# Cross-attention and a 16-expert feed-forward layer on one core: fewer early weight pieces per batch, the last batch's add moved up, b2 copies written as flat runs

## The chip, the cores and the metric

One Trainium2 chip, one of its cores. The metric is the device time of one execution in microseconds, the median of several runs. A core has five engines: TensorE (PE in the profile, its weight loads PEld), VectorE (DVE), ScalarE (ACT), GpSimd (POOL) and SyncE (SP), which here only issues transfers; 16 DMA engines move the data.

## The reference

Eight batches of 100 tokens of width 512, a context of 722 rows for each batch, everything in float32:

```
x = x + attend(layernorm(x), ctx)      # attend: h = gelu(x ctx^T) * (x ctx^T), then h ctx
n = layernorm(x)
e = argmax(n @ router_w), gate = sigmoid(logit of e)          # one expert of 16 for a token
x = x + gate * (gelu(n @ w1[e] + b1[e]) @ w2[e] + b2[e])
```

w1 is 16 x 512 x 1024, w2 is 16 x 1024 x 512: 4 MB an expert, 64 MB in all.

## The kernel before

**Attention stage.** A loop over the eight batches b. Each has its context in two layouts, transposed (`ctxT_a`, `ctxT_b`) and plain (`ctx_main`, `ctx_rest`), each cut into two parts: the first 384 rows (chunks 0 to 2) and the other 338 (chunks 3 to 5). Parts are numbered n = 2b and 2b + 1 and rotate through three places for each layout in the tile `area`. TensorE runs for a batch: `hidden` (L319, six chunks), in between the transposes and logits of the batch before (L341, L347), its routing (L354, L355, L359), then `attention` (L331, three matmuls of the first part, three of the second) and, between these, the transposes of the next normalised x (L308). VectorE adds the residual (`add_x2`, L549), takes its statistics (`x2_stats`), and routes. When a batch is routed, GpSimd writes its rows to memory (`put_rows`, L813).

**Transfers.** SyncE issues nearly all of them from one queue in the order of its program; a wait on it holds back all that stands behind. In batch b it waits for the places of the two transposed parts 2b + 3 and 2b + 4 (L227), of the plain parts 2b + 3 (L234 to L236) and 2b + 4 (L231), and of x of batch b + 3 (L218). Between these it issues pieces of the weights of the first four experts, which have places of their own (`W_early`) and wait for nothing: a piece is half of w1 or of w2 of an expert, 1 MB, 8 KB in each of 128 partitions (`load_w`, L242); 16 of them make up four experts, taken in order from the iterator `early`, two in each batch. In batch 1 it also issues b1 and the four b2 copies (L276): `b2_q`, a table of 4 x 16 x 129 floats in memory, each of its four quarters read into 32 partitions of `b2s`. The fifth place for weights lies in `area` and is filled after the last context; experts 5 to 15 follow as places come free (`s_w1_used` and so on).

**Expert stage.** Work comes in units of 32 tokens of one expert. The first four units ("early", experts 0 to 3) are chosen after batch 6; their rows are gathered from memory by GpSimd (L869), signalled by `s_er[0]` to `s_er[3]`. Then each expert has one unit that always runs (`must`) and as many more as it needs (`more`, a loop over a count read at run time). For a unit VectorE normalises and transposes the rows (`fetch`, L664 to L669), TensorE runs `first_layer` (L376, 32 matmuls; L385), VectorE turns the result and adds b1 (`turn`, L692, `add_bias`, L697), ScalarE applies gelu (L495), TensorE runs `second_layer` (L398, 64 matmuls), VectorE finishes (L685) and GpSimd scatters the rows (L826). The order on VectorE around the first units is written out by hand: wait for `s_tab_e`, `s_bias` and `s_er[0]`, `fetch` of unit 0, then `add_x2` and `x2_stats` of batch 7, then `turn` of unit 0. On TensorE: `first_layer` of expert 0, the transposes and logits of batch 7, `first_layer` of expert 1, and so on.

Of the kernel before, what the change touches and what calls it, by code (L numbers as in the profile page):

```python
# [14 lines left out]
P = 128  # L15
NB, T, D, S = 8, 100, 512, 722
E, F = 16, 1024
# [8 lines left out]
U = 32  # L26
# [50 lines left out]
def build(nc, x, ctx_main, ctx_rest, ctxT_a, ctxT_b, router, w1, b1, w2, b2, consts, out):  # L77
    rows = nc.dram_tensor("rows", (TOK, Q * ROW), F32).ap()
    rows_q = rows.rearrange("n (j c) -> (n j) c", c=ROW)
    b2_q = nc.dram_tensor("b2_q", (Q, E, P + 1), F32).ap()  # L80
    out_q = out.rearrange("b t (j d) -> (b t j) d", j=Q)

    with ExitStack() as stack:
        def sb(name, shape, dt=F32):
            return stack.enter_context(nc.sbuf_tensor(name, shape, dt))
# [11 lines left out]
        b1s, b2s = sb("b1s", [P, E, KF]), sb("b2s", [P, E, P + 1])  # L97
# [38 lines left out]
        def ctxT_part(n):  # L136
            at0, w = PART * (n % 3), (SA, S - SA)[n % 2]
            return area[:, at0:at0 + KD * w].rearrange("p (k s) -> p k s", k=KD)

        def ctx_part(n):  # L140
            at0 = PART * (3 + n % 3)
            return area[:, at0:at0 + PART].rearrange("p (c d) -> p c d", c=3)
# [72 lines left out]
        @block.sync  # L215
        def _(sp):
            def load_x(b):
                sp.dma_start(xin[0:XS, b % XR, :], x[b][0:XS]).then_inc(s_x[b % XR], 16)  # L218
                if b == 0:
                    return  # L220
                load_x_rest(b)

            def load_x_rest(b):
                sp.dma_start(xin[XS:T, b % XR, :], x[b][XS:T]).then_inc(s_x[b % XR], 16)

            def load_ctxT(n):
                sp.dma_start(ctxT_part(n), (ctxT_a, ctxT_b)[n % 2][n // 2]).then_inc(s_T[n % 3], 16)  # L227

            def load_ctx(n):
                if n % 2 == 0:  # L230
                    sp.dma_start(ctx_part(n), ctx_main[n // 2][:, 0:3, :]).then_inc(s_C[n % 3], 16)  # L231
                else:
                    rest = ctx_rest[n // 2]
                    sp.dma_start(ctx_part(n)[:, 0:2, :], ctx_main[n // 2][:, 3:5, :]).then_inc(s_C[n % 3], 16)  # L234
                    sp.dma_start(ctx_part(n)[0:CS, 2, :], rest[0:CS]).then_inc(s_C[n % 3], 16)
                    sp.dma_start(ctx_part(n)[CS:CW[-1], 2, :], rest[CS:CW[-1]]).then_inc(s_C[n % 3], 16)  # L236

            def load_w(e, piece):
                w, src = (W1, w1) if piece < 2 else (W2, w2)
                n = (KD, KF)[piece // 2] // 2  # L240
                h = piece % 2
                sp.dma_start(w[e % SLOTS][:, n * h:n * h + n], src[e][:, n * h:n * h + n]  # L242
                             ).then_inc(s_w[e % SLOTS][piece], 16)

            sp.dma_start(con[:, 0:C_ONE], consts[:, 0:C_ONE]).then_inc(s_con0, 16)
            load_x(0)
            load_ctxT(0)
            sp.wait_ge(s_zero, 2)
            load_x_rest(0)
            load_ctxT(1)  # L250
            load_ctx(0)
            load_ctx(1)
            load_x(1)
            sp.dma_start(con[:, C_ONE:C_ALL], consts[:, C_ONE:C_ALL]).then_inc(s_con, 16)
            for k in range(KD):
                sp.dma_start(rw[U * k:U * k + U], router.rearrange("(g r) k e -> k r g e", g=Q)[k]).then_inc(s_con, 16)
            sp.dma_start(b2_q[:, :, 0:P], b2.rearrange("e (j d) -> j e d", j=Q)).then_inc(s_b2q, 16)
            sp.dma_start(b2_q[:, :, P:P + 1], consts[0:Q, C_ONE:C_ONE + E].unsqueeze(2),
                         allow_slow_non_contiguous=True).then_inc(s_b2q, 16)
            load_ctxT(2)  # L260
            load_ctx(2)
            load_x(2)
            early = iter([(e, piece) for e in range(SLOTS - 1) for piece in range(4)])
            for b in range(NB):
                if 2 * b + 3 < 2 * NB:
                    sp.wait_ge(s_xps[0], b + 1)
                    load_ctxT(2 * b + 3)
                load_w(*next(early))
                if 2 * b + 4 < 2 * NB:
                    sp.wait_ge(s_xps[1], b + 1)  # L270
                    load_ctxT(2 * b + 4)
                if b == 1:
                    sp.dma_start(b1s[:, :, :], b1).then_inc(s_bias, 16)
                    sp.wait_ge(s_b2q, 32)
                    for j in range(Q):
                        sp.dma_start(b2s[U * j:U * j + U], b2_q[j].unsqueeze(0).to_broadcast([U, E, P + 1])  # L276
                                     ).then_inc(s_bias, 16)
                if 2 * b + 3 < 2 * NB:
                    sp.wait_ge(s_att0, b + 1)
                    load_ctx(2 * b + 3)  # L280
                load_w(*next(early))
                if 2 * b + 4 < 2 * NB:
                    sp.wait_ge(s_att, b + 1)
                    load_ctx(2 * b + 4)
                if b + 3 < NB:
                    sp.wait_ge(s_x2, b + 1)
                    load_x(b + 3)
            sp.wait_ge(s_xps[1], NB)
            load_w(SLOTS - 1, 0)
            load_w(SLOTS - 1, 1)  # L290
            sp.wait_ge(s_att, NB)
            load_w(SLOTS - 1, 2)
            load_w(SLOTS - 1, 3)
            for e in range(SLOTS, E):
                sp.wait_ge(s_w1_used, e - SLOTS + 1)
                load_w(e, 0)
                load_w(e, 1)
                sp.wait_ge(s_w2a_used, e - SLOTS + 1)
                load_w(e, 2)
                sp.wait_ge(s_w2b_used, e - SLOTS + 1)  # L300
                load_w(e, 3)
# [226 lines left out]
        def _(dve):  # L528
# [16 lines left out]
            def add_x2(b):  # L545
                dve.wait_ge(s_att, b + 1)
                if b > 1:
                    dve.wait_ge(s_row[b % 2], 16 * (b // 2))
                nc.vector.tensor_tensor(xw[:, b % 2, :, 0:P].rearrange("p g (k r) -> p g k r", k=KD),  # L549
                                        xin[0:T, b % XR, :].rearrange("p (k g r) -> p g k r", k=KD, g=Q),  # L550
                                        p_att[0:T, :].rearrange("p (k g r) -> p g k r", k=KD, g=Q), ALU.add
                                        ).then_inc(s_x2, 1)

            def x2_stats(b):
                dve.wait_ge(s_x2, b + 1)
                nc.vector.bn_stats(bn_t[:, :], xw[:, b % 2, :, 0:P]).then_inc(s_bnt, 1)
                dve.wait_ge(s_bnt, b + 1)
                nc.vector.bn_aggr(ag_t[:, :], bn_t[:, :]).then_inc(s_agt, 1)
                dve.wait_ge(s_agt, b + 1)
                nc.vector.tensor_scalar(ve_t[:, :], ag_t[:, 1:2], EPS, None, ALU.add).then_inc(s_vet, 1)  # L560
                nc.vector.tensor_copy(xw[:, b % 2, :, P + 1:P + 2], ag_t[:, 0:1].unsqueeze(1).to_broadcast([T, Q, 1]))
# [58 lines left out]
            def early_slots():  # L620
                first = p_tab.rearrange("p (e n) -> p e n", e=E)[:, 0:EARLY, 0]
                dve.wait_ge(s_tabps, NB - 1)
                nc.vector.tensor_scalar(tab_e[:, :], first, far_col, None, ALU.add).then_inc(s_tab_e, 1)
                nc.vector.tensor_scalar(tab_before, p_tab, far_col, None, ALU.add).then_inc(s_tab0, 1)
# [37 lines left out]
            def fetch(j, v, row, index, e):  # L662

                nc.vector.tensor_scalar(tb[:, :], row[:, 0:P], row[:, P + 1:P + 2], row[:, P + 2:P + 3],  # L664
                                        ALU.subtract, ALU.mult).then_inc(s_tb, 1)
                dve.wait_ge(s_tb, v)
                nc.vector.transpose(xT[:, :], tb[:, :]).then_inc(s_xT, 1)  # L667
                nc.vector.transpose(rT[:, :], row[:, 0:P]).then_inc(s_rT, 1)
                nc.vector.tensor_copy(lin[:, bass.ds(ring(j), 1)], index)  # L669
# [19 lines left out]
            def turn(v):  # L689

                dve.wait_ge(s_h, v)
                nc.vector.transpose(hb0[:, :], p_h[:, 0:KF * U]).then_inc(s_hc, 1)  # L692
# [40 lines left out]
            fix_early()  # L733
            early_slots()

            dve.wait_ge(s_tab_e, 1)
            dve.wait_ge(s_bias, 16 + 16 * Q)
            dve.wait_ge(s_er[0], 16)
            fetch(0, 1, grow[:, 0, :], tab_e[:, 0:1], 0)
            add_x2(NB - 1)  # L740
            x2_stats(NB - 1)
            turn(1)
            residual(0, 1, grow[:, 0, :], 0)
            dve.wait_ge(s_er[1], 16)
# [213 lines left out]
```

## Time and profile before

| | |
|---|---|
| median of 3 runs | 353.48 us (353.39 to 358.01) |
| the profiled execution | 353.11 us, span 351.0 us |
| busy in the span | PE 267.0 us, PEld 199.8, DVE 137.2, ACT 33.4, POOL 97.2 |
| mean granted TensorE clock | 0.909 |
| moved by DMA | 99.72 MB, mean 284 GB/s |
| last attention matmul ends | 130.1 us |
| first expert's first matmul | 138.8 us |
| last transfer of weights issued | 295.1 us |

The profile is of one execution on the chip. All times in it count from the first instruction. Work of an engine that nobody waits for costs nothing, so a row is read together with what it waited for (in brackets) and with the stretch it stands in. A DMA share near 1 means that the 16 engines are full.

### The profile page before, as it was taken

To read this page: it belongs to the slowest core of one execution; us is meant where nothing else is said; L and a number is where in the kernel's file an instruction comes from. 1 tells how busy PE (TensorE), PEld (TensorE's weight loads), DVE (VectorE), ACT (ScalarE), POOL (GpSimd) and SP (SyncE) were. 2 spreads that over 40 slices of the span, in tenths; PEclk is the share of its full clock that TensorE was granted. 3 is DMA by queue.
4 is the path that set the end of the run, shared out by engine and by line. 5 is a ranking of instruction groups with operands and counts; after the bars stand their busy time and mean duration, and the time that the engine had idled before them with its cause. 6 is when DMAs were issued, how large, how long until landed. Compare 5 with 4: busy or idle time off the path is not lost.

```text
span 351.0 us, 10179 instructions
## 1 busy us (share of the span) xinstructions
PE 267.0 (76%) x3996; PEld 199.8 (57%) x3996; DVE 137.2 (39%) x485; ACT 33.4 (10%) x75; POOL 97.2 (28%) x142
## 2 busy tenths in 40 slices
PE   0899959989988981889756869654857869888950
PEld 0867827584764730557635657432646747777740
DVE  3135514352643332566522345220522434455520
ACT  1211111111111100200000000000000000000000
POOL 1002101010210104145443145322151352434431
PEclk9999998988999896898997899898995998999995
DMA  7999999999999998010199973999999989700000
GB/s 258 351 385 358 295 273 378 364 369 363 376 373 370 380 409 349 8 41 16 35 376 413 413 289 133 399 417 416 416 415 412 385 320 419 304 26 19 16 19 6
DMA packets 19729, 99.72 MB, mean 284 GB/s; under 512 B 4081, under 2 KB 4401, under 8 KB 11353
## 3 DMA queue, kind: packets, MB, share of 16 engines
q1 hardware_dynamic: 16920, 93.94, 70.8%
q0 software_dynamic: 2752, 5.03, 4.3%
q8 instruction: 35, 0.57, 0.7%
q14 instruction: 22, 0.17, 0.2%
HBM read 96.23 MB, written 3.82 MB: 285 GB/s over the span
## 4 chain that ended last, share of the span: by engine, by line
PE 53%; DMA 20%; issue 13%; DVE 6%; SPq 3%; DVEq 2%; ACT 1%; POOL 0%; POOLq 0%
PE bank L376 20%; PE bank L398 15%; DMA area<-in_ctx_rest 9%; PE bank L319 7%; PE bank L331 7%; DMA area<-in_ctxT_b 4%; PE bank L385 2%; DMA rows<-xw 2%; DMA first_area<-in_router 2%; DMA grow<-rows,tab_e 2%; DMA grow<-rows,from_now 2%; DVE tb L664 1%; DVE hb L692 1%; DVE xT L667 1%; PE bank L347 1%
## 5 line engine op out<-in xcount | busy, mean ns | idle before, releaser
L376 PE MATMUL bank<-W_early,xT 128*32 128x256 f32 x800 | 59.3, 423 | 34.7 <-issue 19.9
L398 PE MATMUL bank<-W_early,hT 128*32 128x128 f32 x1600 | 64.0, 289 | 14.1 <-issue 11.9
L398 PEld LDWEIGHTS bank<-W_early,hT 128*32 128x32 f32 x1600 | 52.7, 117 | 20.7 <-issue 17.9
L376 PEld LDWEIGHTS bank<-W_early,xT 128*32 128x32 f32 x800 | 32.7, 119 | 53.7 <-issue 27.9
L331 PE MATMUL bank<-area,hidT 128*100 128x512 f32 (+1 forms) x96 | 49.1, 652 | 6.2 <-DMA area<-in_ctx_rest 6.2
L319 PE MATMUL bank<-xnT,area 128*128 128x100 f32 (+1 forms) x384 | 50.0, 284 | 2.6 <-DMA area<-in_ctxT_b 2.1
L319 PEld LDWEIGHTS bank<-xnT,area 128*128 128x128 f32 (+1 forms) x384 | 47.0, 196 | 6.6 <-issue 5.7
L826 POOL DMA_INDIRECT out<-y,at x32 | 34.2, 1068 | 27.3 <-POOL at L823 23.0
L692 DVE STREAM_TRANSPOSE hb<-bank 128x256 f32<-128x256 f32 x32 | 14.4, 450 | 64.3 <-PE bank L376 57.5
L331 PEld LDWEIGHTS bank<-area,hidT 128*100 128x100 f32 (+1 forms) x96 | 16.4, 184 | 27.3 <-issue 20.4
L495 ACT ACTIVATE hT<-hb 128x256 f32<-128x256 f32 x32 | 13.3, 416 | 176.2 <-PE bank L398 152.7
L685 DVE SCALAR_TENSOR_TENSOR y<-bank,res 128x128 f32 (+1 forms) x32 | 11.2, 351 | 37.1 <-PE bank L398 29.5
L808 POOL TENSOR_TENSOR xw<-ve_t,con 100x4 f32<-100x4 f32 x8 | 8.3, 1039 | 59.6 <-DVE ve_t L560 59.6
L549 DVE TENSOR_TENSOR xw<-first_area,bank 100x512 f32<-100x512 f32 x8 | 5.5, 686 | 44.7 <-PE bank L331 44.7
L823 POOL COPY at<-lin 128x1 uint32 (+1 forms) x32 | 6.4, 199 | 57.8 <-DVE y L685 57.5
L376 PE MATMUL bank<-area,xT 128*32 128x256 f32 x224 | 16.1, 425 | 4.9 <-issue 3.1
L837 POOL DMA_INDIRECT first_area<-rows,area x16 | 16.6, 1035 | 10.9 <-issue 6.1
L837 POOL DMA_INDIRECT grow<-rows,from_now x14 | 14.7, 1050 | 11.4 <-POOL from_now L847 10.6
L398 PE MATMUL bank<-area,hT 128*32 128x128 f32 x448 | 16.6, 292 | 0.2 <-issue 0.2
L385 PE MATMUL bank<-con,rT 128*32 128x128 f32 x256 | 16.8, 291 | 0.0
L813 POOL DMA_DIRECT2D rows<-xw x8 | 5.1, 643 | 41.4 <-DVE xw L608 41.4
L398 PEld LDWEIGHTS bank<-area,hT 128*32 128x32 f32 x448 | 14.7, 117 | 0.8 <-issue 0.6
(89 smaller groups left out, 228.9 us busy)
## 6 DMA issues: line engine op xcount, KB each, us to landing
W_early<-in_w SPq DMA_DIRECT2D x52, 1024.0 KB, 11.5
area<-in_w SPq DMA_DIRECT2D x12, 1024.0 KB, 10.9
area<-in_ctxT_a SPq DMA_DIRECT2D x8, 768.0 KB, 14.1
area<-in_ctx_main SPq DMA_DIRECT2D x8, 768.0 KB
area<-in_ctxT_b SPq DMA_DIRECT2D x8, 676.0 KB, 14.7
area<-in_ctx_main SPq DMA_DIRECT2D x8, 512.0 KB
rows<-xw POOLq DMA_DIRECT2D x8, 206.2 KB, 6.7
first_area<-in_x SPq DMA_DIRECT2D x8, 192.0 KB
```

Source lines behind the costliest of these rows:

```text
L319: last = nc.tensor.matmul(bank_c[0:CW[c], at0:at0 + T], ctxT_part(n)[:, k, P * (c % 3):P * (c % 3) + CW[c]], xnT[:, k, :], start=(k == 0), ...
L331: last = nc.tensor.matmul(p_att[0:T, :], hidT[0:CW[c], c, :], ctx_part(n)[0:CW[c], c % 3, :], start=(c == 0), stop=(c == SC - 1))
L376: last = nc.tensor.matmul(p_h[U * q:U * q + U, 0:2 * P], xT[:, U * k:U * k + U], W1[slot][:, k, :].rearrange("p (c q l) -> p q c l", c=KF, ...
L385: last = nc.tensor.matmul(p_r[U * q:U * q + U, 0:P], rT[:, U * q:U * q + U], ident, start=True, stop=True, tile_position=(0, U * q))
L398: last = nc.tensor.matmul(p_y[U * q:U * q + U, 0:P], hT[:, c, :], W2[slot][:, c, P * q:P * q + P], start=(c == 0), stop=(c == KF - 1), til ...
L495: nc.scalar.activation(hT[:, :, :], hb[:, :].rearrange("p (c t) -> p c t", c=KF), ACT.Gelu).then_inc(s_act, 1)
L685: nc.vector.scalar_tensor_tensor(out=y[:, bass.ds(to, P)], in0=p_y[:, 0:P], scalar=res[:, bass.ds(at0 + P, 1)], in1=res[:, bass.ds(at0, P) ...
L692: nc.vector.transpose(hb0[:, :], p_h[:, 0:KF * U]).then_inc(s_hc, 1)
L808: nc.gpsimd.tensor_tensor(dst, ve[:, 0:1].to_broadcast([T, n]), neg_half.to_broadcast([T, n]), ALU.pow).then_inc(s_rs, 1)
L823: nc.gpsimd.tensor_copy(at[par][:, :], lin[:, bass.ds(at0, 1)]).then_inc(s_at, 1)
L826: nc.gpsimd.indirect_dma_start(out_q, bass.IndirectOffsetOnAxis(ap=at[par][:, :], axis=0), y[:, P * par:P * par + P], None, bounds_check=b ...
L837: nc.gpsimd.indirect_dma_start(dst, None, rows_q, bass.IndirectOffsetOnAxis(ap=index, axis=0), bounds_check=bound_piece, oob_is_err=False) ...
```

## The change

Three edits. SyncE issues one early piece in each batch instead of two (behind the first transposed part), and the eight that are left, experts 2 and 3, in one go behind the loop over the batches, before it waits for the place of the fifth expert. VectorE does `add_x2(NB - 1)` and `x2_stats(NB - 1)` ahead of its waits for `s_tab_e`, `s_bias` and `s_er[0]` instead of behind `fetch` of unit 0. The b2 copies name the same bytes with source and destination as one flat run of 2064 floats instead of 16 by 129.

```diff
 # SyncE
                     for j in range(Q):
-                        sp.dma_start(b2s[U * j:U * j + U], b2_q[j].unsqueeze(0).to_broadcast([U, E, P + 1])
+                        sp.dma_start(b2s[U * j:U * j + U].rearrange("p e c -> p (e c)"),
+                                     b2_q[j].rearrange("e c -> (e c)").unsqueeze(0).to_broadcast([U, E * (P + 1)])
                                      ).then_inc(s_bias, 16)
                 if 2 * b + 3 < 2 * NB:
                     sp.wait_ge(s_att0, b + 1)
                     load_ctx(2 * b + 3)
-                load_w(*next(early))
                 if 2 * b + 4 < 2 * NB:
                     sp.wait_ge(s_att, b + 1)
                     load_ctx(2 * b + 4)
                 if b + 3 < NB:
                     sp.wait_ge(s_x2, b + 1)
                     load_x(b + 3)
+            for e, piece in early:
+                load_w(e, piece)
             sp.wait_ge(s_xps[1], NB)
             load_w(SLOTS - 1, 0)
             load_w(SLOTS - 1, 1)
 # VectorE
             fix_early()
             early_slots()
 
+            add_x2(NB - 1)
+            x2_stats(NB - 1)
             dve.wait_ge(s_tab_e, 1)
             dve.wait_ge(s_bias, 16 + 16 * Q)
             dve.wait_ge(s_er[0], 16)
             fetch(0, 1, grow[:, 0, :], tab_e[:, 0:1], 0)
-            add_x2(NB - 1)
-            x2_stats(NB - 1)
             turn(1)
```

## Rows read from the trace of the kernel before

**Rows 1.** Windows; last columns: granted clock, DMA share, GB/s.

```profile
...
69.00:87.00 18.00, 16.86 (x85) 11.85 (x84) 6.74 (x26) 2.03 (x5) 2.21 (x3) 0.81 1.02 369
139.00:175.00 36.00, 31.37 (x596) 22.31 (x592) 21.99 (x79) 4.48 (x9) 13.85 (x20) 0.89 0.10 31
...
```

**Rows 2.** Waits of TensorE, 9 to 139 us: us in total, times, longest.

```profile
...
PE bank L331 <- DMA area<-in_ctx_rest: 6.2, 3, 4.1
PE bank L319 <- DMA area<-in_ctxT_b: 2.1, 2, 1.1
...
```

**Rows 3.** Timeline of TensorE, batches 1 to 7.

```profile
...
24.37 1.03 PE L319 MATMUL bank<-xnT,area 128*128 128x100 f32 x8
...
51.66 4.49 PE L331 MATMUL bank<-area,hidT 128*100 128x512 f32 x6 [4.06 <-DMA area<-in_ctx_rest]
...
69.48 1.03 PE L319 MATMUL bank<-xnT,area 128*128 128x100 f32 x8
...
74.55 2.82 PE L319 MATMUL bank<-xnT,area 128*128 128x100 f32 x16 [1.14 <-DMA area<-in_ctxT_b]
...
117.24 1.03 PE L319 MATMUL bank<-xnT,area 128*128 128x100 f32 x8
...
127.37 2.74 PE L331 MATMUL bank<-area,hidT 128*100 128x512 f32 x6
```

**Rows 4.** Chain of waits; SyncE's timeline; DMA issues at 103 us.

```profile
...
34.86 16.76 DMA area<-in_ctx_rest
...
59.31 15.11 DMA area<-in_ctxT_b
...
103.06 0.33 SPq L227 DMA_DIRECT2D area<-in_ctxT_b  x1
...
area<-in_ctxT_b SPq DMA_DIRECT2D x1, 676.0 KB, 16.5
```

**Rows 5.** Windows around the b2 copies; page, part 2.

```profile
...
31.00:39.00 8.00, 8.00 (x38) 4.47 (x35) 3.23 (x10) 1.18 (x3) 0.79 (x1) 1.00 1.02 375
39.00:47.00 8.00, 8.00 (x58) 6.20 (x57) 5.16 (x24) 1.27 (x4) 2.21 (x3) 1.00 1.05 197
...
DMA packets 19729, 99.72 MB, mean 284 GB/s; under 512 B 4081, under 2 KB 4401, under 8 KB 11353
...
```

**Rows 6.** Timeline of GpSimd and TensorE; DMA issues from 45 to 46.

```profile
...
125.61 0.61 POOL L813 DMA_DIRECT2D rows<-xw  x1 [5.21 <-DVE xw L608]
...
132.25 1.12 POOL L869 DMA_INDIRECT grow<-rows,tab_e  x1 [6.04 <-DMA rows<-xw]
...
138.78 3.64 PE L376 MATMUL bank<-W_early,xT 128*32 128x256 f32 x32 [8.67 <-DVE xT L667]
...
151.08 1.93 PE L376 MATMUL bank<-W_early,xT 128*32 128x256 f32 x32
...
rows<-xw POOLq DMA_DIRECT2D x1, 206.2 KB, 8.0
```

**Rows 7.** Timeline behind the first expert's fetch.

```profile
...
138.87 0.68 DVE L549 TENSOR_TENSOR xw<-first_area,bank 100x512 f32<-100x512 f32 x1
...
142.48 0.45 DVE L692 STREAM_TRANSPOSE hb<-bank 128x256 f32<-128x256 f32 x1 [1.73 <-PE bank L376]
...
142.77 0.93 PE L341 MATMUL bank<-con,xw 100*128 100x100 f32 x4
...
```

**Rows 8.** Page, part 3; TensorE's waits, 175 to 303.5; VectorE's timeline.

```profile
...
q8 instruction: 35, 0.57, 0.7%
...
PE bank L376 <- issue: 23.0, 12, 4.8
...
173.03 0.34 DVE L664 TENSOR_SCALAR tb<-first_area 128x128 f32<-128x128 f32 x1
...
303.47 0.35 DVE L664 TENSOR_SCALAR tb<-grow 128x128 f32<-128x128 f32 x1 [0.72 <-issue]
...
331.20 0.35 DVE L664 TENSOR_SCALAR tb<-first_area 128x128 f32<-128x128 f32 x1
...
```

## The prediction

> **What bounds the kernel now.** I read the stages first, by windows. Through the attention stage the 16 DMA engines are full (share 1.02 and 1.05) [rows 1, 5]; at the start of the expert stage they fall idle for over 30 us (share 0.10 from 139 to 175) [rows 1]. So there are two stages with two limits, and the question is which waits end last in each. The waits of TensorE up to 139 us are context transfers, 6.2 + 2.1 us [rows 2], and each drags TensorE's clock down: after the 4.06 us wait the six attention matmuls took 4.49 us where an undisturbed batch takes 2.74, and the batch with the 1.14 us wait ran at a granted clock of 0.81 over 18 us, between the levels 1.2 and 2.4 GHz, which is 3.4 us lost [rows 1, 3]. An undisturbed batch lasts 127.37 + 2.74 - 117.24 = 12.87 us [rows 3]; the transfers need longer: the second transposed part of a batch landed at 59.31 + 15.11 = 74.42 and three batches later at 103.06 + 16.5 = 119.56, so 15.05 us a batch [rows 4]. The attention stage is bound by DMA by 2.2 us a batch. The expert stage isn't: no row names a wait for a weight; its pace is TensorE's, and I come back to it below.
>
> **Part 1: one early piece a batch, eight behind the last context.** A piece is 1024 KB, 1.05 MB; at the 375 GB/s of an undisturbed stretch [rows 5] it takes 2.8 us of all 16 engines. Taking one piece out of a batch leaves 15.05 - 2.8 = 12.25 us of transfers against 12.87 us of TensorE: the limit changes hands, by only 0.6 us a batch.
> *Ceiling.* Batch 1 starts at 24.37; seven batches of 12.87 end at 114.5, where now the last attention matmul ends at 130.1 [rows 3]. At most 15.6 us are won.
> *What stays of the stalls.* The longest wait (batch 2) is for the transfer issued at 34.86, landed at 51.62; TensorE wanted it at 51.66 - 4.06 = 47.6 [rows 3, 4]. In front of it in SyncE's order stand two early pieces of batches 0 and 1 that stay, one that goes, and the b2 copies. One piece less: it lands at 48.8, and 1.2 us of wait stay. The clock loss behind it I bound by 0 and by the 3.4 us above, and take the 1.75 us (4.49 - 2.74) of the same place. Later batches: the part for batch 4, landed at 74.42, has three pieces less before it, so 66.0; batch 4 would start at 24.37 + 3 x 12.87 + 1.2 + 1.75 = 65.9 and want it 3.9 us in (74.55 less its wait of 1.14 is 73.41; the batch started at 69.48 [rows 3]), at 69.8. The margin grows by 0.6 us a batch, so no other wait is left.
> Attention: 15.6 - 1.2 - 1.75 = **12.6 us** won (11.0 to 15.6).
> *What the moved pieces meet.* The engines have the same bytes to move and a queue that stays filled (12.25 us of work against 12.87 eats 0.6 us a batch from a queue over 15 us deep), so they end at the same time as now, about 139 us. From the last batch's row write (125.61) to the first expert's matmul (138.78) runs a chain of its own: write lands, gather issued at 132.25, gather lands, VectorE, TensorE after 8.67 us idle [rows 6]. It ran under full engines before and does again, so it moves up unchanged: first expert at 126.2. Experts 2 and 3 need their weights 12.3 us behind the first (151.08 [rows 6]), at 138.5: the eight pieces are issued in one go behind the last context, which lands at about 119.56 - 6 x 2.8 (its transposed part) + 4.6 (a piece and the part itself, 1.74 MB at 375 GB/s) = 107.4; the next piece ends at 110.2 and expert 2's four at 121.4, 17 us early. No wait. SyncE's later waits (for slot 4) stand in the same order; what queues behind the eight issues, at 0.43 us each, is nothing that is due.
> *The price.* The first 13 us of the expert stage (126.2 to 139) now run beside full DMA engines, where before they ran beside idle ones. What that does is seen later in the same stage: from 173.03 to 303.47, with full engines for most of it, 19 units took 6.87 us each; from 303.47 to 331.20, with idle ones, six took 4.62 [rows 8]. The difference isn't weights. TensorE waits "for nothing that the profile shows", up to 4.8 us at a time, 12 times in front of L376 alone, in the middle of runs of matmuls; 35 packets of 16 KB bring instructions over the same 16 engines [rows 8]. I read it as code that comes late. Two units and a bit are exposed: bounds 0 (straight code, fetched ahead) and 2.3 x 2.2 = 5 us. These units are straight code and have other chains beside them (6 us apart even with idle engines, rows 6: 138.78 to 151.08 for two), so I am nearer to the low end: **+1.5 us**. The last batch's row write, 150 us now, falls at about the end of the full stretch; its reader comes ten microseconds later: 0.
> The Trainium skill, page "Runtime: NRT & Kernel Launch", section "Instruction fetch mechanics", says that the next block of instructions is fetched while the current one runs and that only a taken branch forces a wait; by it these straight units would cost nothing. The loops later in the trace agree with its second half; no row of full engines beside straight expert code exists.
>
> **Part 2: VectorE adds x2 of the last batch ahead of the wait for early rows.** The add (0.68 us at 138.87) and its statistics stood between two waits; behind them VectorE idles 1.73 us for TensorE's first layer at 142.48, and TensorE's transposes of x2 start at 142.77, right behind matmuls of its own order, not waiting for x2 [rows 7]. So an earlier x2 feeds nobody: 0. Could it cost? The moved add waits for the last attention matmul, and the row fetch stands behind it on VectorE. That matmul ends at about 117.6, the early rows land at about 125.4: covered by 8 us. GpSimd's root is queued behind its four gathers either way. I take 0, bounds -0.5 to +0.5 (a third of its 1.7 us either way).
>
> **Part 3: b2 copies in long runs.** The copies are dear: in the eight microseconds in which they move the engines carried 197 GB/s, full, against 375 before [rows 5]; 8 x 178 GB/s = 1.4 MB, 3.8 us. Would longer runs cure it? If each of the 4 x 32 rows moved as 16 runs of 516 B, 2048 packets would lie between 512 B and 2 KB; the page counts 4401 - 4081 = 320 there [rows 5]. So they are in long runs already, and the slowness is of another kind (all 128 rows read four short stretches of memory). I take 0; if I am wrong, 3.8 us of DMA time ahead of the 1.2 us wait: the wait and its clock loss go, -2.95.
>
> **Sum.** 353.1 (profiled execution; span 351.0) - 12.6 + 1.5 + 0 + 0 = 342.0; the median of the runs stands 0.4 above the profiled one: **342.4 us**, -3.1%.
>
> **Rivals.**
> *A, everything hides:* no wait left in batch 2, or b2 faster, and straight code that isn't held up: 353.5 - 15.6 = 337.9 (338 to 340.5 with either half). For it: the margin missing is only 1.2 us. Against: the count of packets. 0.22. The skill's rule on instruction blocks alone gives 342.4 - 1.5 = 340.9 and belongs here.
> *B, full engines slow the first experts as they do the later ones, or the clock falls again in a batch:* +5 for 1.5, 3.4 for 1.75: 347.5. For it: 6.87 against 4.62. 0.18.
> *C, the contexts stay the limit:* the 0.6 us margin a batch is thin; if the rate without the pieces is nearer to the 369 GB/s of another stretch [rows 1] and landing order costs more, a wait of 0.5 to 1 us a batch and its clock loss stay; some 5 us less won: 348. 0.08.
> *D, slower than before:* GpSimd's transfers queue behind the nine pieces. If they did, the row write at 113 would land with the last piece at 139 instead of 119.4, the gathers behind slot 4's pieces as well: first expert at about 147, 8 us later than now: 362. It decides as soon as queues are served in order of issue. Against it: a row write issued between 45 and 46 us landed after 8.0 us [rows 6] while the context part issued at 34.86 had taken 16.8 [rows 4]. The skill, page "DMA: Bandwidth & Descriptors", section "Queues, rings and completion order", says that an engine takes turns between the queues; the 8.0 us agree. 0.04.
>
> **How the numbers follow.** My forecast (341 to 344.5) holds 0.48, A 0.22, B 0.18, C 0.08, D 0.04. Range 337.5 to 347.5: it takes in A and most of B. 2% of 353.5 is 7.1 us, about what a measurement of this kernel can tell from no change, so the border is 346.4: faster 0.48 + 0.22 + half of B and a little of C = 0.83, slower 0.04 (D), within 0.13.
>
> **What would show it.** Right: PE windows of 12.87 us a batch from batch 3 on; one context wait in the stage, of about 1.2 us at 47.6; the last attention matmul near 117.6; the 8 us idle in front of the first expert unchanged; DMA share 1.0 until about 139 and its idle stretch shorter at its front end by 12 us; page counts of packets under 2 KB and the 197 GB/s unchanged. Wrong: context waits in batches 3 to 7 (C), units 0 to 2 longer than 6.3 us with new issue idle (B), row writes above 8 us (D).

## The result and the profile after

| | before | changed |
|---|---|---|
| median of the runs of this comparison | 355.75 us (353.39 to 509.57, n 4) | 339.44 us (338.48 to 344.77, n 4) |
| profiled execution | 353.11 us, span 351.0 | 339.28 us, span 337.1 |
| mean granted TensorE clock | 0.909 | 0.939 |

The ratio is 0.9554, 95% interval 0.9437 to 0.9671: faster by more than the 2% that a measurement of this kernel can tell. It leaves out executions in a slower state of the chip, as the one of 509.57 us. On another chip the same kernel later had 0.9641 (0.9559 to 0.9724). Of the 353.5 us these ratios are 15.8 and 12.7 us, and the two profiled executions are 13.9 us of span apart; 11.1 had been forecast. Chips differ (before: 347.8, 353.4 and 355.2 us on the three chips of the experiments), so times are compared on one chip, by their ratio to the kernel before.

The waits of TensorE up to 139 us, the answer to [rows 2]: us in total, times, longest.

```profile
engine line waited for: us in total, times, longest us
PE bank L310 <- DVE first_area L544: 9.4, 1, 9.4
PE bank L378 <- DVE xT L669: 9.0, 1, 9.0
PE bank L333 <- DMA area<-in_ctx_rest: 1.5, 1, 1.5
```

Of the 8.3 us of context waits one of 1.5 us is left. TensorE's timeline around it, answering to [rows 3]:

```profile
49.70 2.82 PE L333 MATMUL bank<-area,hidT 128*100 128x512 f32 x6 [1.53 <-DMA area<-in_ctx_rest]
52.36 1.03 PE L321 MATMUL bank<-xnT,area 128*128 128x100 f32 x8
...
65.18 1.03 PE L321 MATMUL bank<-xnT,area 128*128 128x100 f32 x8
...
103.66 1.03 PE L321 MATMUL bank<-xnT,area 128*128 128x100 f32 x8
...
113.79 2.74 PE L333 MATMUL bank<-area,hidT 128*100 128x512 f32 x6
```

Read there: the matmuls behind the wait take 2.82 us, full pace, where those behind the 4.06 us wait of before took 4.49; batches 3 to 6 take 12.82 us each ((103.66 - 52.36) / 4); the last attention matmul ends at 116.5, 13.6 us earlier. The windows, answering to [rows 1] (last columns: granted clock, DMA share, GB/s):

```profile
69.00:87.00 18.00, 18.00 (x118) 13.15 (x118) 10.64 (x44) 2.65 (x7) 2.82 (x4) 1.00 1.03 347
117.00:126.00 9.00, 0.47 (x8) 0.24 (x12) 2.25 (x9) 0.00 (x0) 5.20 (x5) 0.58 1.01 415
126.00:139.00 13.00, 11.92 (x204) 7.84 (x200) 8.23 (x34) 2.81 (x5) 0.84 (x2) 0.90 1.00 412
139.00:159.00 20.00, 16.26 (x390) 12.25 (x384) 11.49 (x40) 1.25 (x3) 11.61 (x16) 1.00 0.18 59
```

TensorE is now never idle from 69 to 87 us and its clock stays at its upper level, where it was 0.81 in the mean; the engines stay full until 139, right through the first units of the expert stage. GpSimd's timeline, answering to [rows 6], and VectorE's at the first unit that reads the last batch's rows:

```profile
112.03 0.61 POOL L815 DMA_DIRECT2D rows<-xw  x1 [5.21 <-DVE xw L610]
118.78 1.12 POOL L871 DMA_INDIRECT grow<-rows,tab_e  x1 [6.15 <-DMA rows<-xw]
...
136.00 0.66 POOL L815 DMA_DIRECT2D rows<-xw  x1 [11.07 <-DVE xw L610]
```

```profile
145.74 0.35 DVE L666 TENSOR_SCALAR tb<-first_area 128x128 f32<-128x128 f32 x1 [0.45 <-DMA first_area<-rows,area]
```

The row write at 112 us, under full engines, takes what it took before (6.5 us for 6.4), so the eight pieces in one go don't hold it up. The last batch's, at 136, now runs beside full engines too. Before, at 150 us, it landed in 2.7 us and the first gather of its rows was issued 4.4 us behind it; now that gather is issued 7.1 us behind it, at 143.07. (The profile names no landing for this write; in pieces_only and after_again below the same write took 6.2 and 6.3 us.) For the first time VectorE waits for what comes of it, 0.45 us.

Where the 13.9 us of span went, by the starts of VectorE's fetches (L664, now L666; units counted from 0). Beside it stand two kernels of the experiments, both profiled on one chip: b2_only, which is the kernel before with the b2 copies in their other notation, and pieces_only, the same kernel as before with the moved pieces alone.

```
stretch                          before   after    diff.     b2_only  pieces_only  diff.
up to the first fetch            138.03   124.78   -13.25     137.92       125.25  -12.67
units 0 to 2                      16.06    15.31    -0.75      15.90        15.03   -0.87
units 3 to 6                      23.83    22.76    -1.07      19.21        21.21   +2.00
units 7 to 30                    153.28   154.49    +1.21     152.42       153.13   +0.71
from unit 31's fetch to the end   19.80    19.76     0         18.25        18.68   +0.43
```

The two pairs agree on the first two rows and not on units 3 to 6. (Batch 1 began 3 us later in b2_only than in pieces_only; in add_only it began earlier still, and its first fetch is at 138.08 all the same.) There the profile of before isn't typical: its unit 3 (from fetch to fetch) took 9.3 us, with TensorE's matmuls in short pieces (last section), against 4.9 in b2_only and in add_only, which run the same code in those units; together units 3 to 6 take 19.2 and 19.5 us in these two. In the profiles of the changed kernel and its variants they take 21.2 to 24.8 us, where the engines empty at 139. In the pair of b2_only and pieces_only TensorE is busy for the same 15.94 us in these units, and the 2.0 us lie in VectorE's waits for gathered rows and the work behind them, first b2_only, then pieces_only:

```profile
DVE tb L665 <- DMA grow<-rows,from_now: 2.2, 1, 2.2
```

```profile
DVE tb L665 <- DMA grow<-rows,from_now: 3.4, 1, 3.4
DVE tb L665 <- DMA first_area<-rows,area: 0.6, 1, 0.6
```

So the change has a price of about 2 us behind its gain of 12.7, and the first pair hides it by chance. The differences of the last two rows are no larger than those between executions of one kernel (the changed kernel's units 7 to 30 took 154.5 and 153.2 us in its two profiles).

### The profile page after: what moved, and what is told of

It reads as the page before. It is cut to its first block, busy times and chain, and to the rows that moved or that the text cites. A ratio compares the mean times of both kernels' runs of the same rounds, so it can differ in the third digit from the quotient of the medians.

```text
span 337.1 us, 10179 instructions
## 1 busy us (share of the span) xinstructions
PE 256.5 (76%) x3996; PEld 190.3 (56%) x3996; DVE 137.0 (41%) x485; ACT 33.4 (10%) x75; POOL 97.2 (29%) x142
## 2 busy tenths in 40 slices
DMA packets 19728, 99.72 MB, mean 296 GB/s; under 512 B 4080, under 2 KB 4400, under 8 KB 11352
## 4 chain that ended last, share of the span: by engine, by line
PE 59%; issue 15%; DMA 12%; DVE 6%; POOL 2%; DVEq 1%; SPq 1%; POOLq 0%; ACT 0%
PE bank L378 19%; PE bank L400 13%; PE bank L321 11%; PE bank L333 8%; DMA area<-in_ctx_rest 4%; DMA rows<-xw 3%; DMA grow<-rows,from_now 3%; PE bank L387 2%; DMA grow<-rows,tab_e 2%; PE bank L349 1%; DVE tb L666 1%; PE bank L343 1%; DVE xT L669 1%; POOL first_area L839 1%; DVE hb L694 1%
## 5 line engine op out<-in xcount | busy, mean ns | idle before, releaser
L378 PE MATMUL bank<-W_early,xT 128*32 128x256 f32 x800 | 57.0, 412 | 37.6 <-issue 22.9
L378 PEld LDWEIGHTS bank<-W_early,xT 128*32 128x32 f32 x800 | 29.6, 116 | 58.2 <-issue 31.3
L321 PE MATMUL bank<-xnT,area 128*128 128x100 f32 (+1 forms) x384 | 49.3, 281 | 0.6 <-ACT xnT L478 0.6
L333 PE MATMUL bank<-area,hidT 128*100 128x512 f32 (+1 forms) x96 | 44.0, 594 | 1.5 <-DMA area<-in_ctx_rest 1.5
L333 PEld LDWEIGHTS bank<-area,hidT 128*100 128x100 f32 (+1 forms) x96 | 14.8, 167 | 18.8 <-issue 17.0
L839 POOL DMA_INDIRECT first_area<-rows,area x16 | 16.8, 1048 | 13.9 <-issue 8.8
L400 PE MATMUL bank<-area,hT 128*32 128x128 f32 x448 | 16.1, 274 | 1.9 <-issue 1.8
L378 PE MATMUL bank<-area,xT 128*32 128x256 f32 x224 | 14.5, 396 | 3.0 <-issue 2.7
L387 PE MATMUL bank<-con,rT 128*32 128x128 f32 x256 | 16.7, 287 | 0.0
L400 PEld LDWEIGHTS bank<-area,hT 128*32 128x32 f32 x448 | 13.7, 110 | 3.1 <-issue 3.1
```

The source lines that it names most:

```text
L321: last = nc.tensor.matmul(bank_c[0:CW[c], at0:at0 + T], ctxT_part(n)[:, k, P * (c % 3):P * (c % 3) + CW[c]], xnT[:, k, :], start=(k == 0), ...
L333: last = nc.tensor.matmul(p_att[0:T, :], hidT[0:CW[c], c, :], ctx_part(n)[0:CW[c], c % 3, :], start=(c == 0), stop=(c == SC - 1))
L378: last = nc.tensor.matmul(p_h[U * q:U * q + U, 0:2 * P], xT[:, U * k:U * k + U], W1[slot][:, k, :].rearrange("p (c q l) -> p q c l", c=KF, ...
L387: last = nc.tensor.matmul(p_r[U * q:U * q + U, 0:P], rT[:, U * q:U * q + U], ident, start=True, stop=True, tile_position=(0, U * q))
L400: last = nc.tensor.matmul(p_y[U * q:U * q + U, 0:P], hT[:, c, :], W2[slot][:, c, P * q:P * q + P], start=(c == 0), stop=(c == KF - 1), til ...
L839: nc.gpsimd.indirect_dma_start(dst, None, rows_q, bass.IndirectOffsetOnAxis(ap=index, axis=0), bounds_check=bound_piece, oob_is_err=False) ...
```

## The experiments

**The three edits alone**, on one chip (before: 347.79 us).

```diff
 # pieces_only: the changed kernel with edits 2 and 3 undone
 # add_only: the kernel before, and
+            add_x2(NB - 1)
+            x2_stats(NB - 1)
             dve.wait_ge(s_tab_e, 1)
...
-            add_x2(NB - 1)
-            x2_stats(NB - 1)
 # b2_only: the kernel before, and
-  b2s[U * j:U * j + U], b2_q[j].unsqueeze(0).to_broadcast([U, E, P + 1])
+  b2s[...].rearrange("p e c -> p (e c)"), b2_q[j].rearrange("e c -> (e c)")...
```

> The kernel before with the first edit alone (one piece a batch, eight behind the last context). My theory: this edit is the whole change. It gives the changed kernel's time, 339.4 us within 1, with the last attention matmul at 116.5 and one context wait of about 1.5 us in batch 2. Rival (the b2 form or the moved add carry part of it): the time lies between, 341 us or more, and the context wait of batch 2 is longer than 2.5 us or the first expert starts later than 126.5.

Measured: 335.59 us, ratio 0.968 (0.9623 to 0.9738); context waits of 0.7 and 0.2 us, last attention matmul at 116.75, first expert at 126.0. The absolute time was forecast for the chip of the first comparison and is not met; the ratio, which is what can be compared, lies inside the interval of the whole change's second ratio (0.9641) and 0.001 outside that of its first (0.9554). With the two edits below at nothing, the first edit is the change.

> The kernel before with the second edit alone (x2 of the last batch ahead of the wait for early rows). My theory: 0, within 0.3%; x2 is ready 9 us earlier and nobody takes it, the transposes of x2 start behind the first expert's matmuls as before, 4 us behind their start. Rival (an earlier x2 shortens the last batch's routing): the second unit's fetch starts up to 1 us earlier and the time falls by up to 1 us. Rival (the moved add holds up the fetch): plus 0.7 us.

Measured: 347.77 us, ratio 0.9991 (0.9937 to 1.0046). Nothing. The second unit took 9.6 us instead of 6.2 in its profile, which neither theory has; its window shows why, and that no wait is behind it (the last three columns are granted clock, DMA share, GB/s):

```profile
143.00:148.00 5.00, 4.42 (x36) 2.92 (x40) 2.32 (x11) 1.56 (x3) 0.00 (x0) 0.50 0.02 7
```

TensorE ran at its lower level, 1.2 GHz (granted clock 0.50), for the second unit too. It had been idle for about 9 us before the first unit and started it at the lower level in every profile (3.2 to 3.6 us for 32 matmuls that take 1.93 later). In ten of the fourteen profiles the second unit took 6.2 to 6.7 us, in add_only, b2_wide, all_behind and filler 9.6: 3 us more.

> The kernel before with the third edit alone (b2 copies named as flat runs). My theory: the same transfers, so 0 within 0.3%, the page's count of packets under 2 KB stays at 4401 or 4400, and the rate from 39 to 47 us stays near 200 GB/s. Rival (the form was costly): the rate there rises to about 375 GB/s, the context wait of batch 2 falls from 4.1 us to nearly 0 and the time falls by 3 to 4 us.

Measured: 346.54 us, ratio 1.0046 (0.9985 to 1.0107); the wait of batch 2 is 4.1 us as before. The page and the window in which the copies move (4 us later here, for the first batch was slow) settle it:

```profile
DMA packets 19728, 99.72 MB, mean 290 GB/s; under 512 B 4080, under 2 KB 4400, under 8 KB 11352
```

```profile
43.00:51.00 8.00, 8.00 (x60) 6.30 (x59) 5.34 (x25) 1.50 (x4) 2.21 (x3) 1.00 1.03 199
```

4400 - 4080 = 320 packets between 512 B and 2 KB, as in [rows 5]: the same transfers in another notation, at 199 GB/s where it was 197.

**Why the b2 copies are slow.** Two kernels on the changed one.

```diff
 # b2_own_rows: 32 different rows of w1 as the source
-  b2_q[j].rearrange("e c -> (e c)").unsqueeze(0).to_broadcast([U, E * (P + 1)])
+  w1[j][U * j:U * j + U].rearrange("p k f -> p (k f)")[:, 0:E * (P + 1)]
 # b2_wide: one transfer into 128 partitions in place of four into 32 (the loop over j goes)
+  b2s[:, :, :].rearrange("p e c -> p (e c)"), w1[0].rearrange("p k f -> p (k f)")[:, 0:E * (P + 1)]
```

> The changed kernel, its four b2 copies reading 32 different rows of w1 each (8256 B in a row, as before) in place of one stretch of b2 32 times; the bias of the second layer is thus not b2. Same packets, same destination. Theory (the slowness comes from all 32 rows of a copy reading the same 8 KB of memory): the rate in the 8 us of the copies rises from about 215 to 340 GB/s or more, the context wait of batch 2 (1.5 us) goes, and the time falls by 1.5 us. Rival (it comes from the destination, 32 partitions at a time): the rate stays near 215 GB/s, the wait stays at 1.5 us, the time is unchanged.

Measured: 336.43 us, ratio 0.9704 (0.9616 to 0.9792), on the chip of pieces_only (0.968); a wait of 1.17 us in batch 2. The window of its copies, and below it that of b2_wide:

```profile
39.00:47.00 8.00, 8.00 (x59) 6.30 (x58) 5.26 (x24) 1.38 (x4) 2.21 (x3) 1.00 1.03 224
```

```profile
39.00:47.00 8.00, 8.00 (x61) 6.58 (x60) 4.43 (x15) 1.42 (x4) 1.59 (x2) 1.00 1.02 377
```

The theory of the shared source falls: 224 GB/s with a row of its own for every partition, 217 in the same window of the changed kernel.

> The changed kernel with one transfer of 8256 B a row into all 128 partitions of b2s in place of four into 32 partitions each; the source is w1 of expert 0, one row a partition, so the second layer's bias isn't b2. Same bytes and packets. Theory (32 partitions at a time is what makes the copies slow): the rate between 39 and 47 us rises from about 215 to over 340 GB/s, the context wait of batch 2 goes, 1.5 us less. Rival (8256 B runs as such, or what else runs there, are slow): the rate stays near 215 and the wait near 1.5 us.

Measured: 339.27 us, ratio 0.9532 (0.9445 to 0.9619) beside 0.9641 of the changed kernel on the same chip, intervals that overlap. The rate is 377 GB/s and no context wait is left, but neither can be set beside the two profiles above as it is. In this execution batch 1 began at 28.37 us and not at 24.5 to 24.9 (last section), which gives the transfers 4 us more. The profiles of filler and slot4_later began batch 1 as late (28.68, 28.38), have the four b2 copies unchanged in their place, and have no context wait either; so the wait's absence is no work of the wide transfer. The rate can be compared with theirs, here slot4_later:

```profile
39.00:47.00 8.00, 8.00 (x61) 6.57 (x59) 4.44 (x15) 1.43 (x4) 1.59 (x2) 1.00 0.95 267
```

267 GB/s, and 261 in filler, against 377; over the whole stretch in which copies and contexts move, 35 to 53 us, it is 317 and 314 against 343. Same bytes, 48 packets of under 512 B fewer, a source in w1 as in b2_own_rows: what differs is 128 partitions at a time or 32, one transfer or four. By the rates the form of the destination, or the splitting into four, makes the copies slower; how much of the wait it costs isn't shown, nor was it tried how b2 itself could be laid out in one transfer.

**The one wait that is left.** Two kernels on the changed one, on a second chip (before: 355.21 us).

```diff
 # b2_late: b1 and the b2 copies behind the loop
-                if b == 1:
-                    sp.dma_start(b1s[:, :, :], b1).then_inc(s_bias, 16)
-                    ...
+            sp.dma_start(b1s[:, :, :], b1).then_inc(s_bias, 16)
+            ...
             for e, piece in early:
 # second_place: the piece behind the plain part
                     load_ctxT(2 * b + 3)
-                load_w(*next(early))
...
                     load_ctx(2 * b + 3)
+                load_w(*next(early))
```

> The changed kernel with b1 and the four b2 copies issued behind the last context, ahead of the eight pieces. My theory (the one wait left in the attention stage is the b2 copies' doing): the wait of 1.5 us in batch 2 goes, the seven batches take 7 x 12.85 us without a gap, the last attention matmul ends 1.5 us earlier and the time falls by 1.5 us. Rival (the copies hurt wherever they stand): the row write or the gathers of the early rows, which then run near the copies, take longer than 6.5 and 5.9 us, and what was won is given back: 0 or slower.

Measured: 345.59 us, ratio 0.9766 (0.9683 to 0.985). The wait goes and no other appears, as forecast, but batch 1 began at 28.23 us here, where the wait is gone with the copies in their old place too (filler, slot4_later): that part of the theory is untested. The copies now move between 100 and 120 us, in windows of 262 and 272 GB/s, beside the row write, and the rival's part shows in GpSimd's timeline:

```profile
113.55 0.61 POOL L814 DMA_DIRECT2D rows<-xw  x1 [5.21 <-DVE xw L609]
121.63 1.12 POOL L870 DMA_INDIRECT grow<-rows,tab_e  x1 [7.47 <-DMA rows<-xw]
```

7.5 us of wait in place of 6.2; from the last attention matmul (118.06) to the first expert (128.41) it is 10.35 us in place of 9.0. Units 3 to 6 take 24.8 us, with 2.3 and 2.5 us of VectorE's waits for gathers. Late copies cost about as much as they could win.

> The changed kernel with its one piece a batch issued behind the plain context part, where the other one stood, instead of behind the first transposed part. One piece less stands ahead of the transfer that batch 2 waits for, 2.8 us. My theory: the wait of 1.5 us goes and the time falls by 1.5 us; the gain of the change depends on what stands ahead of one transfer. Rival (the wait only moves to the next part, which has the same number of pieces ahead): a wait of about 1 us shows in batch 3 or at the first part of a batch, and the time is unchanged.

Measured: 342.3 us, ratio 0.9671 (0.9574 to 0.9768). The wait of batch 2 goes and comes back in batch 3, at the part that now has the piece ahead of it. TensorE's timeline and the window around it (last columns as above):

```profile
55.51 3.09 PE L321 MATMUL bank<-xnT,area 128*128 128x100 f32 x16 [1.04 <-DMA area<-in_ctxT_b]
```

```profile
54.00:64.00 10.00, 8.96 (x40) 6.68 (x40) 4.94 (x21) 0.92 (x3) 1.16 (x2) 0.66 1.03 343
```

That is the rival, and worse than the wait of the changed kernel: behind a wait of 1.04 us the granted clock is 0.66 over 10 us, and the batch takes 17.31 us (67.86 - 50.55), 4.5 more than its 12.83, while the 1.53 us of the changed kernel cost 0.2 beyond themselves. Batch 1 began at 24.89 here, so the two can be compared.

**How many pieces can go behind, and what full engines cost there.** Same chip as the two above. The changed kernel itself was not run on it, so the ratios are read beside that of second_place (0.9671), and what is late is read in the profiles.

```diff
 # all_behind: no piece in the batches, 16 behind the loop
-                load_w(*next(early))
 # filler: engines kept full behind the fifth expert's pieces
             load_w(SLOTS - 1, 3)
+            for i in range(7):
+                sp.dma_start(filler[i], w1[SLOTS + i][:, 0:2]).then_inc(s_fill, 16)
```

> The changed kernel with all 16 early pieces behind the last context. Attention has then 9.5 us of transfers for 12.85 us of TensorE a batch. Theory: no context wait, so 1.5 us less at the last attention matmul, but the cover is gone: the pieces land from about 104 to 147 us, expert 3's second half at about 145 against a need at 142, so 0 to 3 us come back as waits before L378 or L400 in units 2 and 3; in sum between -1.5 and +1.5 us. Rival (full engines slow early expert code): units 3 to 6, now beside full engines until about 156, take 27 us instead of 22.8 and the time is 3 us or more above.

Measured: 346.11 us, ratio 0.9792 (0.9692 to 0.9892). No context wait, but batch 1 began at 29.00 us, so this shows little; and no row names a wait for a weight. What is late is a gather. VectorE's timeline at unit 4 (its fetch):

```profile
157.39 0.34 DVE L665 TENSOR_SCALAR tb<-first_area 128x128 f32<-128x128 f32 x1 [6.08 <-DMA first_area<-rows,area]
```

> The changed kernel with seven copies of 1 MB from memory to memory (a scratch that nothing reads) issued behind the fifth expert's pieces, which keep the 16 DMA engines full from about 139 to 157 us or longer, where they are idle now. Theory A (straight code isn't held up, loops are): unit 3 unchanged, units 4 to 6 (the first with a loop over a count) go from 17.1 us toward 3 x 6.9 = 20.6 us; total plus 3 us. Theory B (full engines slow all expert code, and the slow first units of the kernel before were their doing as well): units 3 to 6 go from 22.8 to 27.5 us, plus 4.7. Theory C (the 6.9 us pace comes from the weights themselves, not from full engines): units unchanged, plus 0.

Measured: 350.35 us, ratio 0.9837 (0.9676 to 0.9998). The same place. GpSimd's timeline, then VectorE's:

```profile
141.72 0.66 POOL L820 DMA_DIRECT2D rows<-xw  x1 [14.90 <-DVE xw L615]
...
151.28 1.05 POOL L844 DMA_INDIRECT first_area<-rows,area  x1 [5.45 <-issue]
```

```profile
158.29 0.35 DVE L671 TENSOR_SCALAR tb<-first_area 128x128 f32<-128x128 f32 x1 [7.51 <-DMA first_area<-rows,area]
```

The last batch's row write takes 8.8 us to land and the gather behind it 6.9; unit 3 lasts 12.5 us instead of 5.6. None of the three theories had that. The engines stayed full until 161 us (share 0.95 from 157 to 161, 0.76 in the two microseconds behind), so of the units of Theory A only the first 3 us of unit 4 ran beside them: 7.9 us for 7.2, and units 4 to 6 took 16.7 where 17.1 had been the value without filler. That is no test of A. But units 0 and 2 under full engines are as long as before (5.15 and 4.19 us for 5.14 and 4.23), and unit 1 has its 9.6 us of the lower clock, as add_only had beside idle engines; so these units, straight code, aren't held up.

**The tail and the middle**, on a third chip (before: 353.41 us).

> The changed kernel once more, beside the kernel before on this chip: the yardstick for the three others of this call. Profiles of one kernel differ in where TensorE's clock rises: in the first batch (10.5 or 13.5 us from the first to the second) and in the second expert unit (6.2 or 9.6 us). My theory: the ratio to the kernel before is 0.962, within 0.008; a profile that differs from the first one does so in these two places by 3 us each and nowhere else by more than 1. Rival (the time differences of the runs come from memory): the 12.83 us of batches 3 to 7 or the rates above 10 us spread as well.

Measured: 341.1 us, ratio 0.9641 (0.9559 to 0.9724). Batches 2 to 6 took 14.73, 13.04, 13.35, 13.23 and 12.82 us: behind the 1.7 us wait of batch 2 stand two more, of 0.3 and 0.2 us, in batches 4 and 5. The forecast that the batches don't spread holds to 0.5 us. The clock's places are the same in this profile as in the first one.

```diff
 # slot4_later
+            sp.wait_ge(s_must[1], 16)
             sp.wait_ge(s_xps[1], NB)
             load_w(SLOTS - 1, 0)
 # filler_late: behind the last load_w
+            for i in range(12):
+                sp.dma_start(filler[i], w1[i][:, 0:2]).then_inc(s_fill, 16)
```

> The changed kernel with one more wait on SyncE: the four pieces of the fifth expert are issued only once the second gather behind the last batch's row write has landed (about 146 us). Theory (what the moved pieces cost is that this write and these gathers run beside full engines): the engines are idle from about 130, the write lands in 2.7 us instead of 6.8, the first late gather starts 4 us earlier, units 3 to 6 take 21.3 us instead of 22.8: minus 1.5 us, at most minus 3. Rival (that chain isn't the last in these units): 0. Rival (slower: the pieces then fill the engines from 146 to 157 us, under the gathers of the first loop): units 4 to 6 grow, plus 1 to 2 us.

Measured: 344.63 us, ratio 0.9784 (0.9716 to 0.9852), slower than the changed kernel beside it by 1.5%. The mechanism did what was forecast, the time did not: the write lands in 2.7 us, the gather behind it is issued 4.4 us after the write instead of 7.1, VectorE no longer waits for it, and units 3 to 6 still take 24.8 us instead of 22.8. The windows show the pieces where they went (130 to 146 empty, 146 to 159 nearly full):

```profile
130.00:146.00 16.00, 13.65 (x247) 9.07 (x243) 10.55 (x43) 2.81 (x5) 3.96 (x5) 0.93 0.13 44
146.00:159.00 13.00, 9.45 (x227) 7.54 (x221) 6.92 (x23) 1.25 (x3) 7.58 (x10) 1.00 0.88 340
```

The direction is that of the second rival. Its profile is 5.2 us longer than that of after_again: 0.1 up to the first fetch (batch 1 began 3 us later, and the waits and their clock are missing in return), 0.3 in units 0 to 2, 2.0 in units 3 to 6, 2.8 in units 7 to 30. Of units 3 to 6, unit 3 took 7.6 us though nothing kept it waiting for rows; it ran in the same short pieces as unit 3 of before. How the later units come by 2.8 us stays open.

> The changed kernel with twelve copies of 1 MB from memory to memory issued behind the last weights, so that the engines stay full from about 290 to 320 us, where they are idle now. Theory A (the 6.9 us pace in the middle of the expert stage comes from full engines: instruction blocks and gathers come late): units 25 to 30, 28.6 us now, take 6 x 6.5 = 39 us or more, and issue waits of 2 us or longer appear in front of L378; the kernel 10 us slower. Theory B (the pace comes from the weights): these units are unchanged, the kernel at most 2 us slower.

Measured: 350.42 us, ratio 0.9901 (0.9847 to 0.9956), 2.7% above the changed kernel beside it. Windows of the same stretch, first this kernel, then the changed one:

```profile
290.00:320.00 30.00, 21.62 (x502) 15.88 (x505) 11.28 (x39) 2.08 (x5) 10.03 (x16) 0.94 1.01 349
```

```profile
290.00:320.00 30.00, 27.77 (x688) 21.35 (x681) 14.65 (x49) 2.92 (x7) 13.35 (x21) 1.00 0.07 21
```

TensorE is given 502 matmuls in 30 us in place of 688. Units 25 to 30 take 35.3 us in place of 28.6, and of 27.0 in after_again, the yardstick on the same chip. TensorE's waits between 290 and 330 us that no engine and no transfer explains grow from 1.8 and 2.2 us in these two to 8.3, the longest 2.9:

```profile
PE bank L405 <- issue: 5.0, 3, 2.9
PE bank L383 <- issue: 3.3, 4, 1.7
```

No weight is loaded here that anyone waits for. So other traffic by itself slows the expert code with its branches (A), by 1.4 us a unit beside after_again and not the 1.7 forecast; B is out. Whether it is late code, as A reads it, isn't shown: the waits name no cause, and the copies load the memory as well as the engines.

## Why the prediction was right, step by step

- **What bounds attention, and the ceiling.** Right. 12.83 us a batch from batch 3 on, one context wait left of five, the last matmul at 116.5 against 117.6 forecast (batch 1 began 0.6 us later than before, so the seven batches themselves gave 14.2 us). "No other wait is left" holds to two waits of 0.3 and 0.2 us in after_again and one of 0.2 in pieces_only.
- **The wait left in batch 2.** Forecast 1.2 us at 47.6; measured 1.53, ending at 49.7. Its clock loss, taken at 1.75, was 0.2: the low end of its bounds. The two profiles of the changed kernel, b2_own_rows and filler_late have waits of 1.2 to 2.5 us with 0.2 of loss, second_place has 1.04 us with 3.4: the bounds were right, the middle was a guess. The margin is as thin as forecast: where batch 1 begins 4 us later (b2_wide, b2_late, all_behind, filler, slot4_later) there is no wait at all.
- **The chain in front of the first expert moves up unchanged.** Right: 9.0 us of idle against 8.67, and a row write of 6.5 us against 6.4.
- **The weights of experts 2 and 3 are in time.** Right; even with all 16 pieces behind (all_behind) no row names a wait for them.
- **The price of full engines at the start of the expert stage.** This term was mis-sized and put in the wrong place. For late code I added 1.5 us to units 0 to 2; it is 0 (15.3 and 15.0 us against 16.1 and 15.9; unit 2 takes 4.2 us in every profile, unit 0 4.6 to 5.2). By this the trace agrees with the Trainium skill, page "Runtime: NRT & Kernel Launch", section "Instruction fetch mechanics", as far as straight code goes: there the next block of instructions comes while the current one runs. For the last batch's row write I added 0, as falling at the end of the full stretch. It falls inside, the gathers behind it are late, and units 3 and 4 pay: 2.0 us between b2_only and pieces_only, one chip and equal work of TensorE. all_behind and filler, whose engines stay full about 20 us longer, show where this leads: VectorE's wait for the gather is 6.1 and 7.5 us.
- **Why the later units are slow.** That traffic alone, without weights that anyone waits for, slows them is shown by filler_late; its share is about 1.4 us a unit of the 2.2 there, so the rest of the difference between 6.87 and 4.62 has another cause. That the traffic acts through late code stays a reading. More loops and branches lie in that stretch; that was not tried.
- **Edits 2 and 3 at nothing.** Right, both measured alone: 0.9991 and 1.0046. The guess beside it, that the b2 copies are slow because many rows read the same short stretches, is wrong (b2_own_rows).
- **The sum.** 11.1 us were forecast; measured were 12.7 to 15.8 by the ratios, 13.9 in the profiled pair, and 10.4 in the pair of b2_only and pieces_only, where the attention stage gave 12.7. The mechanism is right; that the total comes out so near is in part luck: 1.75 (clock) and 1.5 (code) were too careful, and the 2 us of the late gathers were left out. In rival A one sum is off: with either half alone the time is 339.4 or 340.9, not "338 to 340.5".

Of the rivals, A came closest in time (337.9): no clock loss and straight code not held up, though the wait stayed and the b2 form did nothing. B's slowing exists, but was seen for branching code only. C's waits of 0.5 to 1 us a batch were seen in no profile. D is refuted by the 6.5 us that the row write took though nine pieces were queued.

## What to carry to other kernels

When the transfers of a stage exceed its compute by little, count the bytes that don't have to move in it: taking 1 MB of 5.5 out of each batch moved the limit to TensorE, and the long waits that went also gave back clock. The place to put them is bounded by the next latency chain that starts under them: here the row write and gathers from 136 us on, which cost about 2 us where the engines empty at 139 and a wait of 6 to 7.5 us where they empty at about 160. And before a wait's absence is put down to an edit, look whether the stage began at the same time in both profiles. And look at the packet counts of the page before rewriting an access pattern as a flat run: if they already show the long run, the edit is a change of notation.

## What the hardware showed that was not expected

- While four transfers into 32 partitions each run among the others, the whole window has 197 to 224 GB/s with all engines counted as full, or 261 and 267 where batch 1 began 4 us later (share 0.95); with one transfer of the same bytes into 128 partitions, and batch 1 as late, it has 377.
- TensorE's pace in the first batch differs. Batch 1 begins at 24.4 to 25.6 us in eight profiles and at 28.2 to 29.0 in six, also on one chip (pieces_only and b2_only). The granted clock's record says 1.00 in both, so in this stretch it doesn't tell. The same 24 matmuls in TensorE's timeline, of b2_only and then of the changed kernel, take 5.05 and 2.69 us:

```profile
17.68 5.05 PE L320 MATMUL bank<-xnT,area 128*128 128x100 f32 x24
```

```profile
16.90 2.69 PE L321 MATMUL bank<-xnT,area 128*128 128x100 f32 x24
```

- With the second unit's clock (6.2 or 9.6 us) this can make executions of one kernel differ by some 3 us, nearly 1%. A difference of 1 us between two profiles of this kernel says nothing unless a row is found for it.
- In the profile of before, `second_layer` of unit 2, which runs behind the fetch of unit 3, came in pieces of three to six matmuls with gaps of 0.3 us between, beside idle DMA engines (from 155.1 us on, for example the row below). The same happened in slot4_later, in a weaker form in the changed kernel's next unit (from 145.1 us on), and not at all in b2_only and add_only, which run the code of before: there its 64 matmuls took 1.93 us without a gap. Its cause stays open. With it unit 3 of before is 4.4 us longer than theirs, enough to hide the price of the change.

```profile
155.89 0.43 PE L398 MATMUL bank<-W_early,hT 128*32 128x128 f32 x5 [0.33 <-issue]
```
